# Copying out and rescaling a two-bank running sum: one pair-wide ScalarE instruction each, in place of one per bank

## The reference, cut to what matters

```python
for W in (W_mlp1, W_mlp2, W_mlp3):
    h = SILU_2MOM * silu(h @ W / sqrt(W.shape[0]))
w1, w2, w3, w4 = split(h @ W_mlp4 / sqrt(64), 4, axis=-1)
s0, s1 = x0[sender], x1[sender]
p1 = w1 * s0 * y0
p2 = (w2 * s0)[:, :, None] * y1[:, None, :]
p3 = w3[:, :, None] * s1 * y0[:, None, :]
p4 = w4 * einsum('eum,em->eu', s1, y1) / SQRT3
msg0 = segment_sum(concatenate([p1, p4], -1), receiver)
msg1 = segment_sum(concatenate([p2, p3], 1), receiver)
```

## Time and profile before

| | us |
|---|---|
| median of 3 runs (lowest, highest) | 1435.27 (1434.62, 1439.81) |
| the profiled execution: its time | 1440.99 |
| the profiled execution: its span | 1439.1 |
| PE busy in the span | 1353.6 (94%) |
| DVE busy | 1151.2 (80%) |
| ACT busy | 1003.0 (70%) |
| POOL busy | 922.4 (64%) |

### The profile page before, as it was taken

How to read it: one execution, slowest core, us unless ns; L and a number is a source line. 1 busy time by engine, 2 the same in 40 slices (tenths; PEclk the granted TensorE clock), 3 DMA queues, 4 the chain that set the end, 5 groups by cost and what they waited for, 6 DMA issues and landing times.

```text
span 1439.1 us, 24478 instructions
## 1 busy us (share of the span) xinstructions
PE 1353.6 (94%) x8774; PEld 833.0 (58%) x8774; DVE 1151.2 (80%) x1459; ACT 1003.0 (70%) x2000; POOL 922.4 (64%) x762
## 2 busy tenths in 40 slices
PE   4957999999899999999999699999999999998999
PEld 3454746888378874888567534434444443336887
DVE  7888927999089972999459769999999999995665
ACT  6237726888178863888457459999999999884433
POOL 4226675888888888888883467777777777762000
PEclk9859999999999999999999999999999999999999
DMA  9429476277827566765622769989999999985421
GB/s 331 155 92 334 134 243 239 37 272 278 294 34 282 187 232 187 281 215 158 182 62 49 238 189 306 306 296 307 309 305 303 307 307 293 294 291 176 144 89 59
DMA packets 91601, 316.54 MB, mean 220 GB/s; under 512 B 23754, under 2 KB 25988, under 8 KB 80859
## 3 DMA queue, kind: packets, MB, share of 16 engines
q1 hardware_dynamic: 45832, 202.57, 37.7%
q0 software_dynamic: 45648, 112.41, 28.7%
HBM read 378.96 MB, written 77.16 MB: 317 GB/s over the span
## 4 chain that ended last, share of the span: by engine, by line
PE 70%; DVE 11%; DMA 8%; POOL 5%; issue 4%; ACT 1%; SPq 0%; DVEq 0%; POOLq 0%; ACTq 0%
PE pair L1599 32%; PE pair L1741 7%; PE pair L1636 4%; PE pair L1761 4%; DMA arena<-node_table,arena 4%; POOL arena L1953 4%; DVE arena L1048 3%; PE pair L1758 3%; PE pair L1855 3%; PE pair L1866 3%; PE pair L1653 3%; PE pair L1703 2%; PE pair L1590 2%; POOL pair_rows L1906 1%; DVE arena L1045 1%
## 5 line engine op out<-in xcount | busy, mean ns | idle before, releaser
L1916 POOL DMA_INDIRECT sorted_edges<-arena x311 | 460.1, 1480 | 104.2 <-issue 96.0
L910 DVE TENSOR_TENSOR weights_hl<-arena,weights_hl 128x1024 fp32r<-128x1024 f32 x342 | 405.3, 1223 | 62.3 <-ACT weights_hl L1242 59.7
L1953 POOL DMA_INDIRECT arena<-node_table,arena x352 | 340.7, 968 | 129.6 <-issue 89.4
L1242 ACT ACTIVATE weights_hl<-arena 128x1024 fp32r<-128x1024 f32 x342 | 351.9, 1060 | 46.6 <-PE pair L1599 46.4
L1599 PE MATMUL pair<-weights_hl,rows_hl 128*128 128x512 f32 x1368 | 325.9, 395 | 4.3 <-ACT weights_hl L1242 3.0
L1048 DVE TENSOR_TENSOR arena<-pair,arena 128x1536 f32<-128x1536 f32 x176 | 307.7, 1748 | 0.0
L1599 PEld LDWEIGHTS pair<-weights_hl,rows_hl 128*128 128x128 f32 x1368 | 251.7, 188 | 69.8 <-DVE weights_hl L910 10.5
L1741 PE MATMUL pair<-arena 64*128 64x512 f32 x704 | 185.3, 634 | 7.2 <-DVE arena L1048 7.0
L1599 PE MATMUL pair<-weights_hl,hidden_hl 128*128 128x512 f32 x684 | 165.7, 395 | 0.0
L1391 ACT ACTIVATE arena<-arena 128x32 f32<-128x32 bf16 x704 | 157.8, 314 | 0.0
L1045 DVE TENSOR_TENSOR arena<-pair,arena 128x512 f32<-128x512 f32 x176 | 120.8, 686 | 29.5 <-PE pair L1741 19.8
(11 more groups left out here) (292 smaller groups left out, 1541.0 us busy)
## 6 DMA issues: line engine op xcount, KB each, us to landing
arena<-in_w SPq DMA_DIRECT2D x73, 2048.0 KB, 8.6
arena<-in_w SPq DMA_DIRECT2D x85, 1024.0 KB, 9.2
sums<-arena SPq DMA_DIRECT2D x88, 512.0 KB, 5.7
other_down<-in_w SPq DMA_DIRECT2D x8, 1024.0 KB, 12.2
arena<-in_v SPq DMA_DIRECT2D x16, 512.0 KB, 4.6
pair_rows<-arena SPq DMA_DIRECT2D x1, 5934.0 KB, 26.2
arena<-pair_rows SPq DMA_DIRECT2D x23, 256.0 KB, 3.9
arena<-node_table,arena POOLq DMA_INDIRECT x352
```

Of the source, the lines that this page charges most:

```text
L910: v.tensor_tensor(out=part[s][:, 1], in0=by_chunk(n)[4], in1=part[s][:, 0].bitcast(F32), op=ALU.subtract).then_inc(v_low, 1)
L1242: a.activation(out=part[s][:, 0], in_=cols, func=ACT.Copy).then_inc(a_high, 1)
L1916: g.indirect_dma_start(out=sorted_edges, out_offset=bass.IndirectOffsetOnAxis(ap=slot_i[:, j:j + 1], axis=0), in_=er[:, j, :], in_offset=N ...
L1953: g.indirect_dma_start(out=row, out_offset=None, in_=table, in_offset=bass.IndirectOffsetOnAxis(ap=senders[:, i:i + 1], axis=0)).then_inc( ...
```

## The change

ACT copies all 1024 columns of `sum_pair` in one instruction and rescales all 1024 in one, after PE has done all sixteen products of the step. PE raises `p_sum` once a step, after c = 3, and waits for `a_kept` once, before c = 0. The counts that DVE, PE and SP wait for are adapted.

```diff
-SUMS = 2
...
-            v.wait_ge(p_sum, SUMS * STEPS)
+            v.wait_ge(p_sum, STEPS)
...
-                for b in range(2):
-                    a.wait_ge(p_sum, SUMS * s + b + 1)
-                    a.activation(out=run_sum[s % NSUM][:, b * 512:(b + 1) * 512], in_=banks[b][:, :],
-                                 func=ACT.Copy).then_inc(a_sum, 1)
-                    if s + 1 < STEPS:
-                        a.activation(out=banks[b][:, :], in_=banks[b][:, :], func=ACT.Copy,
-                                     scale=g_same[:, s + 1:s + 2]).then_inc(a_kept, 1)
+                a.wait_ge(p_sum, s + 1)
+                a.activation(out=run_sum[s % NSUM], in_=sum_pair[:, :], func=ACT.Copy).then_inc(a_sum, 1)
+                if s + 1 < STEPS:
+                    a.activation(out=sum_pair[:, :], in_=sum_pair[:, :], func=ACT.Copy,
+                                 scale=g_same[:, s + 1:s + 2]).then_inc(a_kept, 1)
...
                 for c in range(4):
-                    if s and c < 2:
-                        pe.wait_ge(a_kept, 2 * (s - 1) + c + 1)
+                    if s and c == 0:
+                        pe.wait_ge(a_kept, s)
...
-                    if c in (0, 3):
-                        mm.then_inc(p_sum, 1)
+                mm.then_inc(p_sum, 1)
...
-            pe.wait_ge(a_sum, 2 * STEPS)
+            pe.wait_ge(a_sum, STEPS)
...
-                s.wait_ge(a_sum, 2 * (i + 1))
+                s.wait_ge(a_sum, i + 1)
```

## The result

The changed kernel takes 1440.2 us (17 runs, 1436.02 to 1446.56) against 1435.27 us for the kernel before (17 runs, 1431.41 to 1439.81). The ratio is 1.0032, with a 95% interval from 1.0019 to 1.0046: slower by 2.7 to 6.6 us. A second comparison (11 runs against 22) gave 1.0047 (1.0028 to 1.0065), 1442.18 against 1434.52 us. The forecast was + 0.46 us, "within 0.5%", with a range up to 1440.3. By the first comparison both hold, its median just inside the range. The second median lies 1.9 us above the range, and its interval reaches beyond 0.5%. In the medians some 4.5 to 7 us are there that the sum has not.

What follows compares the result with a forecast made beforehand. PE, DVE and ACT were all within a tenth of full, so the order of waits decides. ACT's shorter work 0, kept sums 0, stage end + 0.46 us: 1435.7 us against the median of 1435.27, range 1431.7 to 1440.3.

Steps and rivals of the forecast that it cites:

- The durations: On ACT, the wide copy was put at 1060 ns and the wide rescaling at 1123 ns, from the L1242 row.
- The kept sums: Rescaled sums reach PE at T + 2.34, before c = 0 at T + 2.77 (shortest T + 2.60): cost 0.
- T: Start of PE's next product after part c = 3 of a step; other times in the step count from it.
- Rivals 1 and 2: Kept sums bind: wide instructions stall, 1444.5 us, chance 0.06; or lost copy overlap costs 80 us, 1516 us, chance 0.01.
- Rival 2: Lost overlap of bank 0's copy with PE's bank 1 products costs 0.92 us a step, 80 us: 1516; chance 0.01.
- ACT's slack: After picks and two activation functions ACT is free at T + 4.87 and waits 0.43 us for the next wide copy.
- The end of the stage: Behind the last product, the wide copy delays PE's transposes and the first loads of stored sums: + 0.46 us, once.
- What PE saves: One wait and one signal less per step in `sum_up`: taken as zero, at most 0.09 us a step.
- rivals 3 and 4: PE gains 0.09 us: 20 times, 1433.9 us, chance 0.07; or in every step, 1427.8 us, chance 0.04.
- three candidates: Possible sources of PE's 0.09 us a step: the second wait, ACT's access to bank 0, or the width itself.
- The store: The store to DRAM starts 0.46 us later, from a ring of three buffers reused 15 us later: cost 0.

Runs made afterwards that it cites:

- mixed kernel: Copies bank by bank as in the kernel before, then one wide rescaling of both banks: 1436.95 us against 1434.52 us, ratio 1.0011.
- before_store_late: Kernel before, with SP's store also waiting for the rescalings: 1615.16 against 1616.44 us where PE's instructions came late; 1442.76 against 1434.83 us in another session.

## Why the prediction was right, and what its sum lacks

**The durations.** Wide copy 1060 forecast, 1023 measured; wide rescaling 1123, 1086. The row of 1024 columns was the right neighbour, 37 ns too high for both although it reads `arena`, which lies in SBUF and not in PSUM, and the measured times are far from the bound of twice the narrow ones.

**The kept sums.** Forecast at T + 2.34 including the way back to PE; measured end of the rescaling T + 2.21, as forecast without the way back. The copy started at T + 0.20 and not at T + 0.13, and the two shorter instructions made up for it. PE started c = 0 at T + 3.03 in that step. PE's waits for the rescaling rose from 0.8 us, once, to 2.6 us, four times. "Hidden, but for a few steps" was right. Rivals 1 and 2, in which these sums bind, did not occur in the sessions that the forecast was about. Rival 2 needed PE to stand waiting at this point in every step, for 80 us in all; the trace has 2.6 us of PE's waits in its place. The advice of the Trainium skill that stands beside it, page "PSUM — Partial Sum Buffer", section "Summary: rules for kernel authors", is to read PSUM during a matmul from another bank and to evacuate promptly, the latter because space is tight. The changed kernel still follows the first half, other than the prediction says: from 1032.07 on ACT reads the two banks of the sums while PE writes weights into others. What it gives up is the copy of bank 0 beside PE's products into bank 1.

**ACT's slack.** Forecast 0.43 us before each wide copy in steps with two activation functions. Measured are 0.66 us at the median of the 61 such steps, and 0.81 us on average over all. Right that ACT has slack, and the slack a quarter of a us larger than forecast.

**The end of the stage.** 0.46 forecast, 0.43 measured. Right.

**What PE saves.** Taken as zero with a bound of 0.09 us a step. Parts c = 0 and c = 1 to 3 take the same time as before: by starts 0.88 and 1.41 us in both kernels (medians), and four regular steps take 20.67 us. So rivals 3 and 4 fall. The 0.09 us were neither the second wait nor ACT's access to bank 0, for both are gone; of the three candidates the width itself is left.

**The store: the step that failed.** The prediction said that the store to DRAM starts 0.46 us later, out of a ring of three buffers, and costed it at nothing because nobody waits for the ring. That is true of the buffers and misses the DMA engines. The earlier trace rows had a DMA share of 0.90 in the very row that I read, and I looked at three engines in it, not at this. DVE depends on gathers that use these engines beside the stores (they land after 3.9 us with small stores, after 5.2 with full ones), and POOL issues them with 0.15 us a step in reserve. The term that was put at 0 is the size of the excess: 7.9 us by the medians for a store 0.60 us later and nothing else (4.4 to 9.5 us by the interval of the ratio), against 4.9 and 7.7 us for the whole change. That the forecast and its range held is luck: the term came out just under 0.5%, it was not foreseen, and the median of the second comparison lies outside the range.

**What stays open.** Why half a microsecond decides, and 2.3 us cost no more. The runs show that a store issued 0.6 or 2.3 us after the last copy costs 0.4 to 0.5% when the DMA share is 0.90, and that the same 0.6 us cost nothing in a session with a share of 0.68. With stores of 32 KB the whole change costs 1.9 us, not clear of nothing. How gathers and stores interleave on the DMA queues, and whether an earlier store would gain, none of the runs shows. That the way leads through DVE's waits for gathers is argued: the mixed kernel has as many of them as the changed one and a ratio of 1.0011. The kernel before with an added wait of SP that delays nothing was not run, so a cost of the edit as such is not told apart from the cost of the delay. Nor is the ratio of the mixed kernel, 0.11% above before with an interval from -0.05% to 0.28%, told apart from no loss or from a small one.

## What to carry to other kernels

A change that takes work off an engine can move the moment at which a transfer starts; ask of each transfer that is moved what else uses the DMA engines in that stretch, even when no instruction waits for the transfer itself. If the row of a stage shows a DMA share of 0.9, a moved store is a term of the sum, and the cheap test is the kernel before with one added wait ahead of the store. An issuing engine with four issues of 1.26 us in a step of 5.17 us belongs to the list of full engines, though its busy time (329 of 456 us) looks harmless: the pauses between its instructions are part of its rate.

## What the runs showed of the hardware that was not expected

- An ACT instruction over two PSUM banks (128x1024 f32) took 1023 ns reading and 1086 ns reading and writing in place, that is 171 and 234 ns less than two instructions of one bank each by the durations of the earlier trace rows. No cost for crossing the border between banks shows in these times.
- The same program on the same chip took 1435 us in one session and 1616 us in another; on two other chips it took 1604 and 1614 us. The difference lies in the edge stage, which takes 626.3 us from the second to the last start of c = 0 in `before_store_late` and 449.4 in the kernel before. PE's instructions arrived there in ones and twos, 8 in 4.7 us in the rows shown, while the DMA engines had a share of 0.68. What makes them late was not found.
- Removing 480 of 512 KB of each store bought 0.47% of the whole. From the second to the last start of c = 0 it took 442.4 us in place of 449.4, and DVE's waits for gathers, 5.2 us in the profile of the kernel before, were gone.
